# Cross attention without mask products: forbidden exponentials cleared after the fact on GpSimd and VectorE

## The chip, the cores and the metric

One core of a Trainium2 chip runs the whole kernel. The metric is the device time of one execution in microseconds. Engines are named as in the profile: PE is TensorE (PEld its weight loads), DVE is VectorE, ACT is ScalarE, POOL is GpSimd, SP is SyncE, whose queue issues nearly all transfers (SPq).

## The reference, cut to what matters

One layer of a decoder on 4 sequences of 1024 rows and 256 columns, f32: windowed self attention, cross attention to 77 context rows, and a quantized feed-forward part, each on the layer-normed input and added to it. The change is in the cross attention (16 heads of 16):

```
q = split(Q @ Wq.T + bq);  k = split(K @ Wk.T + bk);  v = split(V @ Wv.T + bv)
scores = einsum('bhqd,bhkd->bhqk', q, k) * 0.25
scores = where(mask == 0, -inf, scores)          # mask: (1024, 77) integers
out = einsum('bhqk,bhkd->bhqd', softmax(scores), v)
x = x + out @ Wo.T + bo
```

## The kernel before

Attention is cut into 16 jobs, `JOBS`: (self or cross, sequence, half of the heads), written S0a, X0a and so on. A job has two groups g of four heads. A group of a self job is 8 units of 128 keys, a group of a cross job 4 units of 256 queries (the 77 keys lie on the partitions), 64 cross units in all. For each group the kernel does this:

- *max*: a first product of queries by keys (`run_tensor`, L677) with the mask added by a further product with the identity (L679), and VectorE takes the negated row maxima (L1183; L1179 in self jobs). *rows*, *turnm*: the maxima are cut in three bf16 parts, turned, and sent by a transfer into three extra rows of the queries, so that the next product subtracts them.
- *score*: the second product, transposed (keys on partitions). For a unit of a cross job: for each pair z of heads two matmuls (L706) and then a mask product (L709), which adds -1e30 at forbidden places by multiplying `maskt` with the identity. Each unit fills two of the six PSUM banks.
- ScalarE takes the exponential of both banks at once (L978; self L974) into one of three buffers `pt`. In self jobs GpSimd then clears the half that causality forbids with an affine select (L1451); in cross jobs nothing follows.
- *val*: four matmuls with the values and a column of ones (L748; self L737), accumulated in the two remaining banks; then ScalarE moves them out (*evac*, L987), and the sums go through a gather, a reciprocal, a store and a wide load (*gather*, *invert* L1206, *store*, *widen*) to the scaling on VectorE (*scale*, L1216) and the output product (*out*, L759).

No engine chooses its next step at run time. `attention_order` writes one list of steps out by hand: each group has a period of 24.5 (self) or 9.6 (cross) units of planned time, and `PLACE` gives the fractions of the period between which the steps of a kind are spread. Steps that follow another (`follow`) are put `BEHIND` so many steps after it. `val` is put two units behind its score. Each engine runs the steps that concern it in the order of this list and waits on semaphores. `pool_steps` is GpSimd's share of the list, `banks_of` gives PSUM banks in turn, and `read_out` says which semaphore frees a bank. The cross keys and values of the next job are made in a step `xkeys` (L649 on TensorE, L1169 on VectorE, L1446 on GpSimd; the last two wait for the last `val` of the job two places earlier in `JOBS`) and in a `bulk` step of six transfers from `kparts` (L517), both under the place "keys x".

The mask itself is loaded once (*masks*, L1108 to L1113): `maskq` for the first product, and its transpose `maskt` for the second, both with 0 or -1e30.

## Time and profile before

| | us |
|---|---|
| median of 3 runs | 851.69 |
| lowest and highest | 844.95, 858.25 |
| span of the profiled execution | 849.0 |
| busy TensorE, VectorE, ScalarE, GpSimd | 684.6, 545.8, 415.1, 188.8 |
| cross scores run between | 300 and 701 |

The profiled execution is one run with the profiler on; its span goes from its first to its last instruction and no other time of it is given. A matmul's duration in the table is from start to modelled end; consecutive matmuls overlap, so that the start of the next one tells what a matmul holds TensorE for. An idle time is put down to the work that ended it.

### The profile page before, as it was taken

Reading aid. Unit: us, or ns where it says so; the run is one execution under the profiler, and the core shown is the slowest. Engines: PE = TensorE matmul, PEld = TensorE weight load, DVE = VectorE, ACT = ScalarE, POOL = GpSimd, SP = SyncE. Lnnn points to the kernel's source line nnn. Section 1 sums busy time; section 2 is a strip of 40 time slices with the busy share of each in tenths; the row PEclk is TensorE's granted clock in tenths of the full one; section 3 lists DMA queues with packets and bytes.
Section 4 is the critical chain, followed back from the end, with each engine's and each line's share of the span. In section 5 each row is a group of like instructions: output and inputs, shape, how many; then the busy total and the mean of one; then the engine's idle time right before and its main releaser. Section 6 shows DMA issues by size and latency. Waiting matters only on the chain.

```text
span 849.0 us, 14814 instructions
## 1 busy us (share of the span) xinstructions
PE 684.6 (81%) x5391; PEld 414.9 (49%) x5396; DVE 545.8 (64%) x975; ACT 415.1 (49%) x610; POOL 188.8 (22%) x231
## 2 busy tenths in 40 slices
PE   2579999989996998999979989897886784488565
PEld 1346565655653564556644644464543442233254
DVE  6277658866864456677636874556745651679996
ACT  2324665536463444555334446433343352399775
POOL 5002131312231120310113123002002000044436
PEclk9988999999997997999988989997998786699989
DMA  7534243502622153243222432331237112000013
GB/s 215 125 106 143 54 128 81 149 3 90 165 77 61 21 170 105 46 141 78 86 50 96 109 96 69 97 95 42 70 85 211 23 42 53 0 1 2 0 65 135
DMA packets 59557, 71.83 MB, mean 85 GB/s; under 512 B 25003, under 2 KB 36447, under 8 KB 59487
## 3 DMA queue, kind: packets, MB, share of 16 engines
q1 hardware_dynamic: 53391, 68.01, 29.2%
q10 hardware_dynamic: 6096, 2.88, 1.3%
q8 instruction: 44, 0.72, 0.4%
q14 instruction: 26, 0.21, 0.1%
HBM read 17.74 MB, written 4.72 MB: 26 GB/s over the span
## 4 chain that ended last, share of the span: by engine, by line
PE 49%; DVE 22%; issue 8%; ACT 7%; SPq 6%; DMA 6%; ACTq 1%; POOL 1%; POOLq 0%; DVEq 0%
PE banks L630 8%; PE banks L759 7%; PE banks L667 5%; PE banks L737 5%; DVE mneg L1179 4%; PE banks L699 4%; PE banks L640 3%; PE banks L748 3%; SPq L523 3%; PE banks L670 3%; DVE xn L1143 2%; SPq L517 2%; PE banks L706 2%; PE banks L709 2%; DVE tops L1358 2%
## 5 line engine op out<-in xcount | busy, mean ns | idle before, releaser
L1179 DVE TENSOR_REDUCE mneg<-banks 128x4 f32<-128x1024 f32 (+1 forms) x128 | 145.1, 1151 | 68.0 <-PE banks L670 67.5
L974 ACT ACTIVATE big<-banks 128x1024 f32<-128x1024 f32 (+1 forms) x128 | 123.0, 974 | 105.4 <-PE banks L699 101.7
L1451 POOL TENSOR_SCALAR_AFFINE_SELECT big<-big 128x512 f32<-128x512 f32 x128 | 83.1, 650 | 391.6 <-ACT big L974 390.9
L978 ACT ACTIVATE big<-banks 77x1024 f32<-77x1024 f32 x64 | 65.3, 1020 | 86.3 <-PE banks L709 81.8
L667 PE MATMUL banks<-big 96*128 96x256 bf16 (+1 forms) x512 | 94.5, 280 | 13.4 <-DMA big<-parts 9.8
L630 PE MATMUL banks<-xnT,weights 128*128 128x512 f32 x192 | 92.9, 617 | 3.9 <-ACT big L978 3.9
L699 PE MATMUL banks<-big 99*128 99x256 bf16 (+1 forms) x512 | 79.3, 280 | 13.3 <-DMA big<-m3t 5.7
L1183 DVE TENSOR_REDUCE mneg<-banks 128x8 f32<-128x616 f32 x64 | 50.3, 793 | 57.7 <-PE banks L679 57.6
L737 PE MATMUL banks<-big 128*17 128x256 f32 (+1 forms) x1152 | 79.0, 366 | 1.0 <-POOL big L1451 0.6
L670 PE MATMUL banks<-causal,identb 128*128 128x256 bf16 x256 | 72.9, 288 | 0.0
L667 PEld LDWEIGHTS banks<-big 96*128 96x128 bf16 x512 | 47.9, 103 | 45.9 <-issue 26.6
L699 PEld LDWEIGHTS banks<-big 99*128 99x128 bf16 x512 | 45.0, 101 | 48.3 <-issue 32.5
L803 PE MATMUL banks<-oe,weights 128*128 128x512 bf16 x187 | 46.8, 394 | 11.0 <-DVE big L1352 4.4
L630 PEld LDWEIGHTS banks<-xnT,weights 128*128 128x128 f32 x192 | 35.7, 197 | 38.1 <-issue 31.4
L677 PE MATMUL banks<-big 96*128 96x77 bf16 x512 | 43.1, 214 | 13.2 <-DMA big<-kparts 9.6
L706 PE MATMUL banks<-big 99*77 99x256 bf16 x256 | 51.1, 282 | 3.1 <-DVE big L1169 1.1
L677 PEld LDWEIGHTS banks<-big 96*128 96x128 bf16 x512 | 35.3, 108 | 32.9 <-issue 19.8
L709 PE MATMUL banks<-maskt,identb 77*77 77x512 bf16 x128 | 50.4, 394 | 0.0
L987 ACT COPY oe<-banks 128x512 f32<-128x512 f32 x64 | 37.2, 585 | 26.8 <-DMA oTx<-oe 10.9
L1224 DVE TENSOR_TENSOR xs<-banks,xs 128x512 f32<-128x512 f32 x32 | 22.1, 689 | 37.6 <-PE banks L759 37.6
L618 PE MATMUL banks<-ident,xn 128*128 128x128 f32 x128 | 23.7, 319 | 23.9 <-DVE xn L1143 23.5
L748 PE MATMUL banks<-big 77*17 77x256 f32 x512 | 42.7, 426 | 0.0
(155 smaller groups left out, 1163.8 us busy)
## 6 DMA issues: line engine op xcount, KB each, us to landing
big<-parts SPq DMA_DIRECT2D x282, 128.0 KB, 2.5
oc<-sums SPq DMA_DIRECT2D x16, 512.0 KB, 4.6
oTs<-oe SPq DMA_DIRECT2D x64, 64.0 KB, 2.3
out_dram<-oTs SPq DMA_DIRECT2D x16, 256.0 KB, 2.1
xs<-in_x_dram SPq DMA_DIRECT2D x3, 1024.0 KB, 5.8
big<-oe SPq DMA_DIRECT2D x32, 64.0 KB, 2.3
oTx<-oe SPq DMA_DIRECT2D x32, 64.0 KB, 2.3
big<-kparts SPq DMA_DIRECT2D x96, 9.6 KB, 1.8
```

Source lines behind the costliest of these rows:

```text
L630: t = e.matmul(bank(p), w[:, i, :], xnT[T][:, i, blk * 512:blk * 512 + 512], start=(i == 0), stop=(i == 1))
L667: e.matmul(bank(p, j)[:, i * 256 + lo * 128:i * 256 + 256], Q[0:96, hh, c * 128:c * 128 + 128], K[0:96, hh, (c - 1 + lo) * 128:(c + 1) * 1 ...
L670: t = e.matmul(bank(p, j).rearrange("p (s n) -> p s n", s=2)[:, :, 128:256], identb[:, :], causal[:, :].rearrange("p (a n) -> p a n", a=1) ...
L677: e.matmul(bank(p, j)[:, i * KX:i * KX + KX], Q[0:96, i, (c + j) * 128:(c + j) * 128 + 128], xks[r][0:96, i, :], start=(i == 0), stop=Fals ...
L699: t = e.matmul(bank(p, i // 2)[:, (i % 2) * 256:(i % 2) * 256 + n], ks[r][0:99, i, j * 128:j * 128 + 128], qs[r][0:99, i, j * 128:j * 128 ...
L706: e.matmul(bank(p, z)[0:KX, i * 256:i * 256 + 256], xks[r][0:99, 2 * z + i, :], qs[r][0:99, 2 * z + i, j * 256:j * 256 + 256], start=(i == ...
L709: t = e.matmul(bank(p, z)[0:KX, :].rearrange("p (i n) -> p i n", i=2), identb[0:KX, 0:KX], keep.to_broadcast([KX, 2, 256]), start=False, s ...
L737: t = e.matmul(acc[:, col // 512][32 * i:32 * i + 17, col % 512:col % 512 + z - a], va[f][:, j, 4 * g + i, :], P[:, i, a:z], start=new, st ...
L748: t = e.matmul(acc[:, j // 2][32 * i:32 * i + 17, (j % 2) * 256:(j % 2) * 256 + 256], xv[r][0:KX, i, 0:17], pt[u][0:KX, i * 256:i * 256 + ...
L974: e.activation(pt[u].rearrange("p (i n) -> p i n", i=4)[:, :, 0:n], pair(p).rearrange("p j (s n) -> p (j s) n", s=2)[:, :, 0:n], ACT.Exp, ...
L1179: e.tensor_reduce(M.rearrange("p (h c) -> p h c", h=4)[:, :, c], pair(p).rearrange("p j (s n) -> p (j s) n", s=2)[:, :, lo * 128:256], AX. ...
L1451: e.affine_select(out=P[:, :, 0:128], in_=P[:, :, 0:128], compare_op=ALU.is_ge, fill=0.0, base=0, pattern=[[0, 4], [1, 128]], channel_mult ...
```

## The change

The mask products of the second cross product go, and the scores of forbidden keys are no longer lowered. The exponentials of forbidden places, which can be large or infinite, are set to zero in the buffer: in two heads GpSimd multiplies the bits as integers with 0 or 1 (`keepi`), in the other two VectorE takes the minimum with 0 or 3e38 (`maskt`, with new contents). GpSimd's product is the score step in its list; VectorE's minimum is a new step "keep", put two steps behind the score. The value product now waits for both. The first product keeps its mask. The place "keys x" moves from before the start of a period to behind it. `keepi` takes 4 KB per partition, and the scratch for transfer descriptors is made smaller.

```diff
-         "bulk x": (0.192, 0.576), ... "keys x": (-0.198, -0.165), ...
+         "bulk x": (0.192, 0.576), ... "keys x": (0.02, 0.06), ...
 BEHIND = {...
-          "wturn": 2, "val": 2}
+          "wturn": 2, "val": 2, "keep": 2}
 def follow(s):
+    if k == "score" and s[1][0] == "x":
+        return ("keep", BEHIND["keep"], ("keep",) + s[1:])
 ...
+        keepi = sb("keepi", [128, S], I32)
 ...
 run_tensor, score:
-                        keep = maskt[0:KX, j * 256:j * 256 + 256].rearrange("p (a n) -> p a n", a=1)
                         for z in range(2):
                             for i in range(2):
-                                e.matmul(bank(p, z)[0:KX, i * 256:i * 256 + 256], xks[r][0:99, 2 * z + i, :],
-                                         qs[r][0:99, 2 * z + i, j * 256:j * 256 + 256], start=(i == 0), stop=False,
-                                         skip_group_check=True)
-                            t = e.matmul(bank(p, z)[0:KX, :].rearrange("p (i n) -> p i n", i=2), identb[0:KX, 0:KX],
-                                         keep.to_broadcast([KX, 2, 256]), start=False, stop=True, skip_group_check=True)
+                                t = e.matmul(bank(p, z)[0:KX, i * 256:i * 256 + 256], xks[r][0:99, 2 * z + i, :],
+                                             qs[r][0:99, 2 * z + i, j * 256:j * 256 + 256], start=(i == 0), stop=True,
+                                             skip_group_check=True)
 run_tensor, val of a cross job:
-                        e.wait_ge(a_exp, n_of["score", job, g, j])
+                        e.wait_ge(p_keep, n_cross[job, g, j])
+                        e.wait_ge(d_keep, n_of["keep", job, g, j])
 run_vector, masks:
-                    e.tensor_copy(maskt[0:KX, :], bank(p).bitcast(BF16)[0:KX, :]).then_inc(d_mask, 1)
+                    e.tensor_scalar(maskt[0:KX, :], bank(p).bitcast(BF16)[0:KX, :], 0.0, BIG, ALU.is_equal, ALU.mult
+                                    ).then_inc(d_mask, 1)
+                    e.tensor_scalar(keepi[0:KX, :], bank(p).bitcast(BF16)[0:KX, :], 0.0, None, ALU.is_equal
+                                    ).then_inc(d_mask, 1)
 run_vector:
+                elif k == "keep":
+                    _, job, g, j = s
+                    P = pt[pt_at[job, g, j]][0:KX, 512:1024].rearrange("p (i n) -> p i n", i=2)
+                    e.wait_ge(a_exp, n_of["score", job, g, j])
+                    e.wait_ge(d_mask, 2)
+                    e.tensor_tensor(P, P, maskt[0:KX, j * 256:j * 256 + 256].rearrange("p (a n) -> p a n", a=1).to_broadcast(
+                        [KX, 2, 256]), ALU.min).then_inc(d_keep, 1)
 run_gpsimd: "score" steps of cross jobs too
                     e.wait_ge(a_exp, n_of[s])
+                    if job[0] == "x":
+                        e.wait_ge(d_mask, 3)
+                        bits = P[0:KX, 0:2, :].bitcast(I32)
+                        keep = keepi[0:KX, j * 256:j * 256 + 256].rearrange("p (a n) -> p a n", a=1)
+                        e.tensor_tensor(bits, bits, keep.to_broadcast([KX, 2, 256]), ALU.mult).then_inc(p_keep, 1)
 kernel:
-    nc = _bacc.Bacc("TRN2", target_bir_lowering=False, num_devices=1)
+    nc = _bacc.Bacc("TRN2", target_bir_lowering=False, num_devices=1, dynamic_dma_scratch_size=1024)
```

## Rows read from the trace of the kernel before

**Rows 1.** The page, parts 1 and 4: busy us and share; the chain by engine.

```profile
PE 684.6 (81%) x5391; PEld 414.9 (49%) x5396; DVE 545.8 (64%) x975; ACT 415.1 (49%) x610; POOL 188.8 (22%) x231
...
PE 49%; DVE 22%; issue 8%; ACT 7%; SPq 6%; DMA 6%; ACTq 1%; POOL 1%; POOLq 0%; DVEq 0%
```

**Rows 2.** Groups by line and shape: count | busy us, mean ns | idle before.

```profile
L1451 POOL TENSOR_SCALAR_AFFINE_SELECT big<-big 128x512 f32<-128x512 f32 x128 | 83.1, 650 | 391.6 <-ACT big L974 390.9
...
L709 PE MATMUL banks<-maskt,identb 77*77 77x512 bf16 x128 | 50.4, 394 | 0.0
...
L1458 POOL TENSOR_TENSOR xs<-xs,big 128x512 f32<-128x512 f32 x16 | 21.1, 1319 | 1.3
```

**Rows 3.** Timeline of TensorE: start us, us, engine, line.

```profile
385.72 0.38 PE L709 MATMUL banks<-maskt,identb 77*77 77x512 bf16 x1
...
385.94 0.38 PE L706 MATMUL banks<-big 99*77 99x256 bf16 x2
```

**Rows 4.** The chain of waits, shares by line, of five stretches in order.

```profile
by line: SPq L523 16.7%; PE banks L667 12.3%; PE banks L630 9.6%; DMA big<-m3t 9.1%; PE banks L706 7.7%; PE banks L748 7.3%; PE banks L709 7.3%; DMA big<-parts 6.5%; PE banks L670 6.1%; PE banks L640 5.3%; issue 2.9%; PE banks L699 2.8%; AC
...
by line: PE banks L759 17.2%; PE banks L748 9.6%; PE banks L667 9.1%; PE banks L640 8.4%; PE banks L706 7.3%; PE banks L709 6.9%; PE banks L737 6.2%; PE banks L618 4.3%; PE banks L670 4.3%; PE banks L630 3.9%; PE banks L677 3.4%; DVE mneg L
...
by line: PE banks L667 11.7%; PE banks L640 10.9%; PE banks L706 10.3%; PE banks L748 10.3%; PE banks L630 10.1%; PE banks L709 9.0%; DMA big<-m3t 8.5%; PE banks L737 7.8%; PE banks L670 6.0%; PE banks L699 3.3%; PE banks L677 3.0%; PE bank
...
by line: PE banks L759 13.1%; SPq L523 12.3%; PE banks L748 8.6%; SPq L517 7.1%; issue 6.2%; PE banks L630 4.9%; PE banks L706 4.1%; PE banks L709 3.9%; DVE xn L1143 3.7%; ACT big L978 3.7%; SPq L535 3.5%; PE banks L677 3.5%; PE banks L679 
...
by line: PE banks L759 14.0%; DMA oc<-sums 12.0%; issue 6.9%; SPq L535 6.3%; SPq L517 4.7%; DMA sums<-ls 4.3%; SPq L523 4.0%; PE banks L706 3.8%; PE banks L709 3.4%; ACT big L978 3.4%; DMA ls<-oe 3.2%; DVE st L1229 3.1%; DMA oTx<-oe 3.0%; A
```

**Rows 5.** Windows: PE, PEld, DVE, ACT, POOL busy us, PE clock, DMA share, GB/s.

```profile
296.00:332.00 36.00, 31.89 (x286) 20.37 (x290) 20.10 (x34) 17.41 (x26) 7.29 (x8) 0.96 0.51 144
370.00:414.00 44.00, 42.42 (x354) 29.17 (x354) 27.40 (x52) 19.56 (x29) 3.57 (x4) 0.96 0.34 93
460.00:494.00 34.00, 31.66 (x290) 20.15 (x286) 25.85 (x45) 16.81 (x24) 8.61 (x8) 0.95 0.36 101
528.00:640.00 112.00, 94.29 (x788) 57.80 (x784) 65.13 (x139) 44.10 (x64) 14.81 (x20) 0.92 0.33 84
640.00:716.00 76.00, 47.57 (x359) 28.05 (x358) 35.86 (x82) 28.63 (x55) 3.54 (x4) 0.77 0.33 83
...
380.00:390.00 10.00, 10.00 (x98) 7.41 (x98) 9.33 (x21) 4.82 (x8) 1.67 (x1) 1.00 0.50 127
```

**Rows 6.** Timeline: cross exponentials (L978) and weight loads of value products (L748).

```profile
301.42 1.02 ACT L978 ACTIVATE big<-banks 77x1024 f32<-77x1024 f32 x1 [2.14 <-PE banks L709]
...
311.45 0.13 PEld L748 LDWEIGHTS banks<-big 77*17 77x17 f32 x8 [0.30 <-issue]
...
693.22 1.01 ACT L978 ACTIVATE big<-banks 77x1024 f32<-77x1024 f32 x1
...
694.28 0.13 PEld L748 LDWEIGHTS banks<-big 77*17 77x17 f32 x8 [0.49 <-ACT big L978]
...
702.47 1.03 ACT L978 ACTIVATE big<-banks 77x1024 f32<-77x1024 f32 x1
...
703.70 0.56 PEld L748 LDWEIGHTS banks<-big 77*17 77x17 f32 x16
```

**Rows 7.** Timeline: two-input operations of VectorE and GpSimd, alone and together.

```profile
326.51 1.22 DVE L1216 TENSOR_TENSOR oTs<-oTs,oc 128x1024 f32<-128x1024 f32 x1
...
638.43 1.71 DVE L1216 TENSOR_TENSOR big<-big,oc 128x1024 f32<-128x1024 f32 x1
...
639.13 2.13 POOL L1458 TENSOR_TENSOR xs<-xs,big 128x512 f32<-128x512 f32 x1
```

**Rows 8.** The table of waits: engine, line, released by: us, times, longest.

```profile
PE banks L677 <- DMA big<-kparts: 9.6, 2, 4.9
...
DVE big L1169 <- PE banks L748: 5.5, 3, 4.2
```

More of the change, by code:

```diff
@@ L43 @@
 BEHIND = {"scaled": 3, "turned": 3, "scaled 4": 0, "split": 1, "vmove": 0, "bulk": 13, "turnm": 3, "evac": 4,
-          "spread": 2, "gather": 2, "invert": 5, "store": 2, "widen": 8, "scale": 8, "wturn": 2, "val": 2}
+          "spread": 2, "gather": 2, "invert": 5, "store": 2, "widen": 8, "scale": 8, "wturn": 2, "val": 2, "keep": 2}
 def follow(s):
@@ L399, in build @@
         land_y = [sem(f"land_y{i}") for i in range(4)]
-        p_set, p_ones, p_mix, p_rstd, p_rstd3, p_one, p_sel, p_shift, p_wend = (
-            sem("p_" + n) for n in ("set", "ones", "mix", "rstd", "rstd3", "one", "sel", "shift", "wend"))
+        p_set, p_ones, p_mix, p_rstd, p_rstd3, p_one, p_sel, p_keep, p_shift, p_wend = (
+            sem("p_" + n) for n in ("set", "ones", "mix", "rstd", "rstd3", "one", "sel", "keep", "shift", "wend"))
         a_wqkv, a_turnw, a_keys, a_xnT, a_p0, a_p1, a_v, a_m3t, a_exp, a_evac, a_wb, a_wT, a_centre = (
@@ L404, in build @@
                                     "centre"))
-        d_set, d_ctx, d_mask, d_keys, d_clear, d_stat, d_ve, d_xn, d_rem, d_p2, d_xv, d_max, d_rows, d_inv, d_scale = (
-            sem("d_" + n) for n in ("set", "ctx", "mask", "keys", "clear", "stat", "ve", "xn", "rem", "p2", "xv", "max",
+        d_set, d_ctx, d_mask, d_keys, d_clear, d_stat, d_ve, d_xn, d_rem, d_p2, d_xv, d_max, d_keep, d_rows, d_inv, d_scale = (
+            sem("d_" + n) for n in ("set", "ctx", "mask", "keys", "clear", "stat", "ve", "xn", "rem", "p2", "xv", "max", "keep",
                                     "rows", "inv", "scale"))
@@ L440, in read_out @@
                     "xkeys": d_xv, "max": d_max, "turnm": a_m3t, "score": a_exp, "out": d_out}[k], {
-                        "turnw": 2 * n, "masks": 2 * n, "keys": 3 * n - 2, "xkeys": 2 * n}.get(k, n)
+                        "turnw": 2 * n, "masks": 3 * n, "keys": 3 * n - 2, "xkeys": 2 * n}.get(k, n)
         def w_done(s):
@@ L1404, in done @@
                 if k == "score":
-                    n -= n_cross[s[1:]]
-                return {"ones": p_ones, "mix": p_mix, "root": p_rstd, "xkeys": p_one, "score": p_sel, "shift": p_shift,
+                    x = n_cross[s[1:]]
+                    return (p_keep, x) if s[1][0] == "x" else (p_sel, n - x)
+                return {"ones": p_ones, "mix": p_mix, "root": p_rstd, "xkeys": p_one, "shift": p_shift,
                         "root3": p_rstd3, "wend": p_wend}[k], {"xkeys": 2 * n, "wend": 2}.get(k, n)
@@ L1422, in run_gpsimd @@
                 e.memset(va[f][:, :, :, 16:17], 1.0).then_inc(p_set, 1)
-            pool_steps = [s for s in plan if s[0] in ("ones", "mix", "root", "xkeys", "shift", "root3", "wend")
-                          or (s[0] == "score" and s[1][0] == "s")]
+            pool_steps = [s for s in plan if s[0] in ("ones", "mix", "root", "xkeys", "score", "shift", "root3", "wend")]
             for before, s in zip([None] + pool_steps, pool_steps):
```

6 lines of the change are left out of this document (4 added, 2 removed), and 2 rows, old and new, of the table PLACE.

## The prediction

> **What bounds the kernel now.** I read the page first: over the whole span TensorE is busy 81%, VectorE 64% and GpSimd 22%, and the chain that ended last is 49% TensorE, 22% VectorE [rows 1]. An average over stages does not say what the cross scores are worth, so I asked for the chain of waits in the five stretches in which cross scores run (296 to 332, 370 to 414, 460 to 494, 528 to 640, 640 to 716 us; 8, 8, 8, 27 and 13 of the 64 units of work, 302 us together). The reader is to see in them that the mask product L709 is 7.3, 6.9, 9.0, 3.9 and 3.4% of the chain [rows 4]: the first three stretches are nearly pure TensorE, the last two are mixed with DMA issues of SyncE (SPq L523, L517, L535) and landings. Then I looked at what is to take the work over: VectorE is busy 174 of these 302 us, and in its fullest 10 us 9.33 [rows 5].
>
> **The change part by part.**
>
> *Mask products removed (TensorE).* The table gives 50.4 us for 128 of them [rows 2], but matmuls overlap: L709 starts at 385.72 and the next matmul at 385.94, so one costs TensorE 0.22 us and all 128 cost 28.2 [rows 3]. Of this only what lies on the chain can shorten the end: 0.073 x 36 + 0.069 x 44 + 0.090 x 34 + 0.039 x 112 + 0.034 x 76 = 2.6 + 3.0 + 3.1 + 4.4 + 2.6 = 15.7 us [rows 4]. Term: -15.7; ends: 0 (everything hidden by the DMA issues that stand in the same chains) and -28.2.
>
> *Clearing on GpSimd, 64 products on 77x512 elements with two inputs from SBUF.* The trace has no integer product. Below stands the select of 512 elements with one input, 0.65 us, above the one two-input operation of 512 elements that was held up, 2.13 [rows 2, 7]. I take the two-input f32 form, 1.26 to 1.32 us [rows 2], since the change has its shape: 64 x 1.3 = 83 us on an engine that is busy 22% [rows 1]. Engine time there costs nothing; what costs is that it stands between the exponential (L978) and the product with the values (L748). That product is issued two units behind its score. Over the 64 pairs of L978 and L748 (first, a tight one and last in [rows 6]; the first load follows 9.0 us after its exponential) I took the time from the exponential's end to the first weight load that uses it: 57 of 64 have over 1.26 us and hide the product, 7 have less, the shortest 0.05 (exponential ends 694.23, load 694.28 [rows 6]). What is missing sums to 4.9 us. Each score shortened by 0.44 takes slack away from the pairs before it (about 1.5 scores lie between): 0.66 less each makes it 9.5. Delays of neighbours overlap, so: +6; ends 0 and 19 (the same sum at 1.95, the price of both halves in a row, below).
>
> *Clearing on VectorE, 64 minima on 77x512.* The row of 1024 columns takes 1.22 us undisturbed [rows 7], so half of it is about 0.69 with its fixed part. They are queued two steps behind the score on VectorE's in-order queue; behind each one wait the maxima (L1183, L1179) for which TensorE's six banks are held. So VectorE's added time counts by stretch. At 0.69 each, with VectorE filled to 0.93 as in its fullest window [rows 5], a stretch needs at least (busy + added)/0.93: 27.5, 35.4, 33.7, 90 and 48 us. Only the third is then over its new length (34.0 - 3.1 = 30.9), by 2.8.
>
> *The two halves at once.* Both wait for the same exponential. What the trace shows of such pairs: VectorE's product of two SBUF tensors took 1.71 instead of 1.22, and GpSimd's addition that began inside it took 2.13 instead of 1.26 [rows 7]: the second one in got through little while the first ran (0.87 of the 1.01 us that they overlap). So a pair that starts together ends after 0.69 + about 0.86 to 1.0 x 1.26, 1.8 to 1.95 us, and whichever was second carries it. I take the mean cost of a minimum to VectorE as up to 1.3, since it is in the middle of other work at 34 of the 64 ends of an exponential and then arrives late, when the product is partly done. At 1.3 the third stretch needs 39.0 (8.1 over), the others still fit: 32.8 against 33.4, 40.6 against 41.0, 107.8 against 107.6, 57 against 73.4. Term for VectorE: +5, between 2.8 and 8.1; ends: 0 and +43, which with the -15.7 makes the +27 of rival 2. The Trainium skill, "SBUF — State Buffer", section "Who interferes with whom", has a rule that speaks against this change: a VectorE instruction with two SBUF inputs and a GpSimd instruction that reads SBUF exclude each other for the whole instruction. By it each pair that meets takes the full sum of both durations, where the rows let some 0.1 us pass, and if all 64 met with VectorE second, rival 2's time would come out. The trace nearly agrees, with 0.87 of 1.01 us.
>
> *Cross keys later.* In the written order the step moves from 0.198 of a period's length (9.6 for cross, 24.5 for self, in the planner's us) before the period's start to 0.02 behind it: 2.1 later beside cross work, 5.3 beside self work. It is queued on four engines. VectorE's L1169 waits for the end of the value products, 5.5 us in its largest group [rows 8]; standing later it waits less, but it is also behind the minima: -1. The six key transfers per group of heads move behind other transfers of SyncE's queue; TensorE waited 9.6 us for such transfers, twice [rows 8]; hidden elsewhere, here by the same 2.1 to 5.3 more each at worst: +1; ends 0 and +7.4. GpSimd now takes cross scores in order, so a small reciprocal root or a shift may stand behind one product: +1 (ends 0, +4). The third mask operation of VectorE in the setup is one of some 0.7 us beside SyncE's loads and TensorE's first jobs: 0. The smaller scratch of DMA descriptors touches no queue of the trace, where all kernel transfers are issued by SyncE and ScalarE: 0.
>
> *Clock.* The granted clock is 0.96, 0.96, 0.95, 0.92 and 0.77 of full speed (means of the levels 2.4 and 1.2 GHz) [rows 5], lowest where TensorE waits most. New waits may cost one more stretch at 1.2 GHz and less work may bring one forward; ±5, in the range only.
>
> **Sum.** 849.0 - 15.7 + 6 + 5 - 1 + 1 + 1 = 845.3 us against the profiled span of 849.0. The three runs have a median of 851.69 and spread from 844.95 to 858.25, so the span lies 2.7 below the median; on the median's footing the sum is 848.
>
> **Rivals.**
> 1. *TensorE alone decides* (the chain's other parts were only filling its gaps): all 28.2 us go, +6 for the tight exponentials, no loss on VectorE: 851.7 - 28.2 + 6 = 829.5. For it: TensorE is busy 248 of 302 us [rows 5]. Against: the last two stretches, 188 of the 302 us, have 3.4 and 3.9% of L709 on the chain [rows 4]. Chance 0.13.
> 2. *VectorE becomes the bound, slower.* Every minimum is held behind the integer product and costs VectorE 1.95, 125 us in all. By (busy + added)/0.93 the stretches become 38.4, 46.2, 44.6, 126.7 and 73.4 us: +2.4, +2.2, +10.6, +14.7, -2.6, together +27.3, so 879. Place: the in-order VectorE queue in front of the maxima; it decides from a mean cost of 1.3 us a minimum. The rule of the Trainium skill, "SBUF — State Buffer", "Who interferes with whom", comes to this if GpSimd always gets in first. For it: two engines released by one semaphore; VectorE already 9.33 of 10 us full. Against: VectorE's waits for TensorE are part of its idle time and many exponentials end when GpSimd could be through before VectorE comes. With an integer product of 2 us instead of 1.3 it comes sooner. Chance 0.22, from 862 up.
> 3. *Nothing moves*: the chains run over SPq and DMA rows as soon as TensorE is shorter: 852 ± 3. Chance 0.13.
> 4. *The change doesn't do what it says*: an integer product that GpSimd executes much slower than the f32 form, 64 times over 3 us, with each value product waiting for it: above 900. Chance 0.02.
>
> **Numbers.** The forecast (0.50) has its own range of 838 to 860. Low end 832 takes in part of rival 1, high end 872 part of rival 2; 2 in 10 are left out. A measurement of this kernel can hardly tell less than 2%, 17 us, from no change. Faster than 834.7: most of rival 1 and a little of the forecast, 0.15. Slower than 868.7: most of rivals 2 and 4, 0.21. Within: 0.64.
>
> **What would show it.** In the profile after: no L709; TensorE's table total for the cross scores down by 50 us, its starts by 0.22 each. GpSimd +64 products of some 1.3 us, its total up by some 83 us. VectorE's minima: 0.69 where alone, up to 1.95 where both run; a mean above 1.3 and more idle time of TensorE behind L1183 and L1179 is rival 2. L748 waiting for GpSimd or for the minimum in some ten of 64 places, about 1 us each, is my second term; none says that slack grew. SPq L517 on the chain says that the later keys cost. I am wrong if the integer product is far from 1.3 us, or if VectorE meets it nearly always.

## The result: 5% slower, and the profile after

| | before | after |
|---|---|---|
| median of 4 runs each, us | 854.65 | 894.54 |
| lowest and highest | 844.95, 858.25 | 893.84, 895.72 |
| span of the profiled execution | 849.0 | 891.7 |
| mean granted clock of the span | 0.911 | 0.864 |

The ratio is 1.050, with a 95% interval of 1.043 to 1.057. The forecast of 848 us (832 to 872) was a little faster than before, and the kernel came out slower. An execution over 1.5% above the fastest of its kernel is left out of every ratio and every difference here, while medians and ranges given in brackets are of all executions.

The page of the kernel after, parts 1 and 2 (busy us and share by engine; tenths in 40 slices), for [rows 1]:

```profile
PE 690.7 (77%) x5263; PEld 413.5 (46%) x5268; DVE 614.0 (69%) x1040; ACT 416.2 (47%) x610; POOL 287.6 (32%) x295
...
PEclk9889999999997988999899799778665755789979
```

TensorE has 128 matmuls less and is busy 6 us longer; VectorE has 68 us more, GpSimd 99. The digits of the clock fall to 5, 6 and 7 from the 29th to the 35th slice. The same line on the page of the kernel before has 6 to 8 from the 31st to the 35th:

```profile
PEclk9988999999997997999988989997998786699989
```

The groups that the change made or touched, kernel after (line engine op, count | busy us, mean ns | idle before and releaser), for [rows 2]:

```profile
L1467 POOL TENSOR_TENSOR big<-big,keepi 77x512 int32<-77x512 int32 x64 | 95.5, 1492 | 169.0 <-ACT big L980 132.5
...
L1196 DVE TENSOR_TENSOR big<-big,maskt 77x512 f32<-77x512 f32 x64 | 57.2, 894 | 14.4 <-ACT big L980 14.4
L750 PE MATMUL banks<-big 77*17 77x256 f32 x512 | 52.8, 501 | 16.2 <-DVE big L1196 12.1
...
L709 PE MATMUL banks<-big 99*77 99x256 bf16 x256 | 49.9, 331 | 5.1 <-DVE mneg L1188 2.9
```

L709 is now the score itself; the mask product behind it is gone. Windows, first the kernel before between its first and its last cross exponential (301.4 to 702.5), columns as in [rows 5]:

```profile
301.40:702.50 401.10, 344.23 (x2855) 209.90 (x2851) 249.46 (x497) 180.05 (x268) 63.96 (x84) 0.90 0.34 89
```

The same of the kernel after, and below it the stretches that hold as many cross units as the five of [rows 5] (8, 8, 8, 27 and 13):

```profile
301.10:743.20 442.10, 348.96 (x2733) 208.68 (x2734) 315.46 (x559) 180.98 (x267) 160.98 (x148) 0.82 0.30 81
296.00:337.00 41.00, 31.19 (x281) 18.97 (x270) 29.21 (x40) 17.39 (x26) 18.92 (x17) 0.90 0.43 124
374.00:422.00 48.00, 41.24 (x354) 28.15 (x355) 36.48 (x64) 19.43 (x30) 16.06 (x13) 0.96 0.32 90
467.00:510.00 43.00, 34.31 (x274) 20.02 (x276) 34.96 (x58) 17.08 (x24) 20.53 (x17) 0.82 0.29 78
544.00:681.00 137.00, 101.48 (x734) 60.58 (x730) 95.44 (x169) 45.62 (x65) 49.67 (x44) 0.75 0.28 74
681.00:758.00 77.00, 50.01 (x323) 27.46 (x323) 46.40 (x90) 28.13 (x54) 32.02 (x20) 0.57 0.28 67
```

This is the whole loss: between the two exponentials 41.0 of the 42.7 us of the spans. The stretches went from 36, 44, 34, 112 and 76 us to 41, 48, 43, 137 and 77. VectorE is not full in any of them: 71, 76, 81, 70 and 60%.

**Where the 41.0 us are.** Length less TensorE's busy time is its idle time: 401.1 - 344.2 = 56.9 before, 442.1 - 349.0 = 93.1 after, +36.3. The other 4.7 is busy time. It hides two large terms. The mean clock tells how long TensorE was granted the lower of its two levels (1.2 instead of 2.4 GHz; a mean of 0.90 is 20% of the time, 0.82 is 36%). From the clock records themselves it is 78.5 us before and 161.5 after. Taking busy time at the lower level as half as much work, the work at full clock fell by 27.3 us, and 32.1 us came back because so much of it ran at the lower clock. So: -27.3 work, +36.3 idle, +32.1 clock.

**What TensorE waits for.** The table of waits of TensorE between the two exponentials, kernel before (engine, line, released by: us, times, longest):

```profile
PE banks L759 <- DVE oTx L1216: 8.6, 2, 8.3
PE banks L687 <- DVE m L1199: 7.2, 6, 2.0
...
PE banks L618 <- DVE xn L1143: 4.7, 8, 1.3
```

And the kernel after:

```profile
PE banks L691 <- DVE m L1211: 20.6, 11, 4.1
PE banks L750 <- DVE big L1196: 12.1, 8, 2.4
PE banks L773 <- ACT big L1009: 8.3, 7, 2.6
PE banks L671 <- DVE mneg L1184: 7.2, 11, 1.2
...
PE banks L750 <- POOL big L1467: 2.9, 2, 1.6
```

All rows of this view added up by the releasing engine: VectorE 30.8 us before, 62.7 after; GpSimd 0 and 3.2; ScalarE 13.2 and 11.3; transfers 11.6 and 10.4. The new idle time is VectorE's (+31.9), and most of it stands in places that the change did not touch. The largest is the transposition of the row maxima (L691, before L687). It needs four small VectorE instructions in a row (two copies and two subtractions of 128x32, each waiting for the one before, L1205 to L1211). Two things delay them. They stand in one queue with the minima, and they are themselves held while GpSimd works: of the 84 of them between the two exponentials, the 21 that began while a two-input GpSimd instruction ran took 0.68 us on average and up to 1.25, the other 63 took 0.22. In sum they took 28.3 us instead of 18.3. The new wait of the value products for the minimum is 12.1 us, 8 times.

**The pairs.** A timeline of the kernel after, the first cross unit (start, us, engine, line):

```profile
301.12 1.02 ACT L980 ACTIVATE big<-banks 77x1024 f32<-77x1024 f32 x1 [1.56 <-PE banks L709]
...
302.28 1.26 POOL L1467 TENSOR_TENSOR big<-big,keepi 77x512 int32<-77x512 int32 x1 [2.22 <-ACT big L980]
302.42 1.67 DVE L1196 TENSOR_TENSOR big<-big,maskt 77x512 f32<-77x512 f32 x1
```

The product comes 0.14 us ahead and takes its 1.26 us; the minimum takes 1.67 instead of 0.68. And a unit of the kernel after in which they do not meet, but the minimum stands behind other work:

```profile
392.08 1.02 ACT L980 ACTIVATE big<-banks 77x1024 f32<-77x1024 f32 x1 [2.52 <-PE banks L709]
...
393.24 1.65 POOL L1467 TENSOR_TENSOR big<-big,keepi 77x512 int32<-77x512 int32 x1 [2.33 <-ACT big L980]
...
393.87 2.15 DVE L1148 TENSOR_SCALAR xn<-xs,mv,rstd 128x256 f32<-128x256 f32 x4
...
395.93 1.22 DVE L1184 TENSOR_REDUCE mneg<-banks 128x4 f32<-128x1024 f32 x1
...
397.06 0.68 DVE L1196 TENSOR_TENSOR big<-big,maskt 77x512 f32<-77x512 f32 x1
397.66 1.22 DVE L1184 TENSOR_REDUCE mneg<-banks 128x4 f32<-128x1024 f32 x1
...
397.89 0.63 PE L750 MATMUL banks<-big 77*17 77x256 f32 x8 [1.48 <-DVE big L1196]
```

The exponential ended at 393.10, the product with the integers at 394.89. The minimum came at 397.06, after a normalisation and a maximum, and TensorE stood 1.48 us for it. Over all 64 minima: 39 took 0.67 to 0.69 us, and 25, all begun while a two-input GpSimd instruction was running, took 1.23 on average and up to 1.76.

### The profile page after: what moved, and what is told of

Its sections match the earlier page's. It is cut to its first block and busy times, and to the rows that moved or that the text cites. A ratio compares the mean times of both kernels' runs of the same rounds, so it can differ in the third digit from the quotient of the medians.

```text
span 891.7 us, 14850 instructions
## 1 busy us (share of the span) xinstructions
PE 690.7 (77%) x5263; PEld 413.5 (46%) x5268; DVE 614.0 (69%) x1040; ACT 416.2 (47%) x610; POOL 287.6 (32%) x295
## 5 line engine op out<-in xcount | busy, mean ns | idle before, releaser
L1467 POOL TENSOR_TENSOR big<-big,keepi 77x512 int32<-77x512 int32 x64 | 95.5, 1492 | 169.0 <-ACT big L980 132.5
L671 PE MATMUL banks<-big 96*128 96x256 bf16 (+1 forms) x512 | 95.9, 284 | 19.4 <-DMA big<-parts 10.4
L634 PE MATMUL banks<-xnT,weights 128*128 128x512 f32 x192 | 95.2, 631 | 0.5 <-DVE big L1159 0.5
L738 PE MATMUL banks<-big 128*17 128x256 f32 (+1 forms) x1152 | 77.2, 357 | 1.3 <-POOL big L1469 0.8
L671 PEld LDWEIGHTS banks<-big 96*128 96x128 bf16 x512 | 47.8, 104 | 54.0 <-issue 28.4
L1196 DVE TENSOR_TENSOR big<-big,maskt 77x512 f32<-77x512 f32 x64 | 57.2, 894 | 14.4 <-ACT big L980 14.4
L750 PE MATMUL banks<-big 77*17 77x256 f32 x512 | 52.8, 501 | 16.2 <-DVE big L1196 12.1
L681 PE MATMUL banks<-big 96*128 96x77 bf16 x512 | 47.6, 229 | 19.6 <-DMA big<-kparts 11.0
L681 PEld LDWEIGHTS banks<-big 96*128 96x128 bf16 x512 | 38.9, 117 | 41.7 <-issue 27.4
L709 PE MATMUL banks<-big 99*77 99x256 bf16 x256 | 49.9, 331 | 5.1 <-DVE mneg L1188 2.9
L683 PE MATMUL banks<-maskq,identb 128*128 128x308 bf16 x128 | 47.0, 371 | 0.0
```

The source lines that it names most:

```text
L634: t = e.matmul(bank(p), w[:, i, :], xnT[T][:, i, blk * 512:blk * 512 + 512], start=(i == 0), stop=(i == 1))
L671: e.matmul(bank(p, j)[:, i * 256 + lo * 128:i * 256 + 256], Q[0:96, hh, c * 128:c * 128 + 128], K[0:96, hh, (c - 1 + lo) * 128:(c + 1) * 1 ...
L681: e.matmul(bank(p, j)[:, i * KX:i * KX + KX], Q[0:96, i, (c + j) * 128:(c + j) * 128 + 128], xks[r][0:96, i, :], start=(i == 0), stop=Fals ...
L738: t = e.matmul(acc[:, col // 512][32 * i:32 * i + 17, col % 512:col % 512 + z - a], va[f][:, j, 4 * g + i, :], P[:, i, a:z], start=new, st ...
L1196: e.tensor_tensor(P, P, maskt[0:KX, j * 256:j * 256 + 256].rearrange("p (a n) -> p a n", a=1).to_broadcast([KX, 2, 256]), ALU.min).then_in ...
L1467: e.tensor_tensor(bits, bits, keep.to_broadcast([KX, 2, 256]), ALU.mult).then_inc(p_keep, 1)
```

## The experiments

"After" and "before" name the two kernels. Each ratio is to before, run on the same chip. The medians of before, counted as said above, were 850.6 us beside e1 to e4, 850.9 beside e5 to e8, 848.3 beside e10 to e13 and 848.9 beside e9 and e14 to e16. First the parts of the change one by one.

**Both clears out** (e1). From after, GpSimd's products and VectorE's minima are left out, and the value product waits for the exponential:

```diff
-        return ("keep", BEHIND["keep"], ("keep",) + s[1:])
+        return None
...
-                        e.wait_ge(p_keep, n_cross[job, g, j])
-                        e.wait_ge(d_keep, n_of["keep", job, g, j])
+                        e.wait_ge(a_exp, n_of["score", job, g, j])
... (and cross scores leave pool_steps)
```

> The changed kernel with both clears left out (the exponentials at forbidden places stay, the value product waits for ScalarE only); mask products gone, cross keys at their new place. Theory Q (the minimum stands late in VectorE's in-order queue and holds the value products): all of the loss goes and the mask products' 15.7 us show, 830 to 840 us, granted clock 0.90 or more. Theory C (less matmul work alone lets the clock fall: half clock 244 us after against 154 before): the clock stays at 0.88 or lower and the time is 865 us or more. Theory K (keys later): 870 us or more, TensorE waiting for key transfers.

Measured: 853.34 us (847.79 to 858.1), ratio 1.003 (0.999 to 1.007). The clears are what makes after slow; without them it is no faster than before, and none of the three numbers expected came true. The forbidden exponentials stay, so the result of e1 and e2 is not the layer's.

**Only the mask products removed** (e2). As the last, with the keys where they were. It keeps two small parts of the change, the third mask operation of the setup and the smaller scratch:

```diff
-         "keys x": (0.02, 0.06)
+         "keys x": (-0.198, -0.165)
```

> As the run before it, with the cross keys back at their old place: nothing but the mask products is taken from the kernel before. Q: within 5 us of the kernel without clears and new keys. K: faster than that one by 10 us or more. C: granted clock under 0.89 and no gain on the kernel before; Q: 12 to 20 us faster than before.

Measured: 847.42 us (842.49 to 850.38), ratio 0.997 (0.993 to 1.001): 3.2 us where 15.7 were forecast, at most 5.8 by the interval. The 12 to 20 us of theory Q did not come. Its window between the two exponentials, in one of its shortest executions (842.6):

```profile
296.90:693.00 396.10, 326.14 (x2728) 199.63 (x2725) 249.03 (x497) 179.64 (x268) 64.25 (x85) 0.87 0.34 90
```

Work at full clock is 26.6 us less than before, as in after. Idle time is 70.0 (13.1 more), and the lower clock takes 99.6 us instead of 78.5, which costs 8.5. So 26.6 us of removed matmuls shorten the stretch by 5.0. TensorE now waits 39.1 us for VectorE instead of 30.8: part of what was work is a wait for the same VectorE results. The lower clock shows in all executions: the mean granted clock of the span was 0.882 to 0.897 in the ten of e2 and 0.897 to 0.919 in the nineteen of before. The chain's 15.7 us were about five times too much, the 28.2 us from the starts about nine times.

**Only the keys moved** (e3). From before:

```diff
-         "keys x": (-0.198, -0.165)
+         "keys x": (0.02, 0.06)
```

> The kernel before with the cross keys at their new place and nothing else. K: 15 us or more slower than before. Q and C: within 7 us of before.

Measured: 848.72, 862.56, 863.17 and 863.42 us. With three of four far above the fourth no ratio is given, and this run decides nothing: it lies between 2 us less and 13 more. No cause is read from its profile, which is of one of the three. The pair above, e1 against e2, has ten executions of each on one chip, and their means differ by 6.6 us, with a 95% interval of some 4 to 9. So in the kernel without mask products and clears the later keys cost some 6 us; in the kernel before it is open.

**Mask products and clears together** (e4). After, with the mask product put back behind each score (the scores are masked twice):

```diff
-                                t = e.matmul(..., start=(i == 0), stop=True, skip_group_check=True)
+                                e.matmul(..., start=(i == 0), stop=False, skip_group_check=True)
+                            t = e.matmul(bank(p, z)[0:KX, :]..., identb[0:KX, 0:KX],
+                                         keep.to_broadcast([KX, 2, 256]), start=False, stop=True, ...)
```

> The changed kernel with the mask products put back beside both clears, which then clear zeros. C: the matmul work holds the clock at 0.90 or more and the kernel is faster than the changed one, under 880 us. Q: the waits stay and 128 products of 0.22 us come on top where TensorE is on the path: 890 to 910 us, clock near 0.87.

Measured: 901.13 us (899.51 to 905.46), ratio 1.059 (1.053 to 1.064): 6.6 over after. The window holds 27 us more work than after, and 73.2 us of idle time instead of 93.1. What the mask products cost in front of the clears is, within the noise, what they cost without them, some 3 to 7 us.

**GpSimd's products alone** (e5; after without the minima; VectorE's two heads stay uncleared):

```diff
-        return ("keep", BEHIND["keep"], ("keep",) + s[1:])
+        return None
...
-                        e.wait_ge(d_keep, n_of["keep", job, g, j])
```

> The changed kernel without the minima (two of four heads keep their forbidden exponentials; the value product waits for GpSimd's product alone). The two clears together cost 41 us (894.5 against 853.3 without them). Theory Q (the minimum's late place in VectorE's in-order queue and the wait on it): most of the 41 is gone, 853 to 865 us. Theory B (the two engines exclude each other while reading SBUF, and VectorE's time grows by the lock): also gone, so this run alone doesn't part them. Theory G (GpSimd's 1.26 us between exponential and value product, with its own in-order queue): over 870 us.

**VectorE's minima alone** (e6; after without the products; GpSimd's two heads stay uncleared):

```diff
-            pool_steps = [s for s in plan if s[0] in (..., "xkeys", "score", "shift", "root3", "wend")]
+            pool_steps = [s for s in plan if s[0] in (..., "xkeys", "shift", "root3", "wend")
+                          or (s[0] == "score" and s[1][0] == "s")]
...
-                        e.wait_ge(p_keep, n_cross[job, g, j])
```

> The changed kernel without the integer products (the other two heads keep their forbidden exponentials). Q: the loss stays nearly whole, 880 to 894 us, since the minimum stands where it stood. B: without GpSimd there is nothing to exclude, 853 to 868 us. G: 853 to 868 us.

Measured: products alone 870.64 us (865.64 to 870.93), ratio 1.022 (1.018 to 1.027), 17.3 over e1. Minima alone 862.66 (859.65 to 870.1), ratio 1.015 (1.008 to 1.023), 9.3 over e1. The two add up to 26.6; together, in after, they cost 41.2. So 14.6 us (13 by the ratios, and some 10 either way) come from their being there at the same time. The group of the minima in the kernel with minima alone:

```profile
L1195 DVE TENSOR_TENSOR big<-big,maskt 77x512 f32<-77x512 f32 x64 | 44.1, 690 | 15.9 <-ACT big L979 15.9
```

The product alone adds no instruction to VectorE, and still VectorE's busy time between the two exponentials grows. The window of e1 and below it that of e5 (columns as in [rows 5], VectorE is the third):

```profile
297.46:707.81 410.35, 332.96 (x2728) 202.38 (x2724) 248.34 (x497) 179.94 (x267) 63.17 (x85) 0.85 0.32 87
297.17:720.87 423.70, 340.27 (x2727) 204.09 (x2724) 266.88 (x497) 179.88 (x267) 145.97 (x148) 0.84 0.32 84
```

The same 497 instructions take 18.5 us more. The four small ones of the row maxima account for 10.0 of it: the 17 of 84 that began while a two-input GpSimd instruction ran took 0.77 us on average, the others 0.22. TensorE's wait for the last of them rose from 7.7 to 15.5 us, and with the minima alone (e6) only to 9.1. Reductions and operations with an input in PSUM kept their times (128x4 from 128x1024: 1.21 us inside and outside). So a good part of the product's price is that it slows what VectorE already had to do; TensorE waited only 5.2 us for the product itself.

**One product for all four heads** (e7), on GpSimd, no minima. It computes the whole result:

```diff
-                    bits = P[0:KX, 0:2, :].bitcast(I32)
+                    bits = P[0:KX, 0:4, :].bitcast(I32)
```

> One integer product of 77x1024 on GpSimd clears all four heads, no minima: the full result. Its duration should be near 2.5 us, twice 1.26. Q: 2.5 us exceed the gap to the value product in about half of the 64 units, but no VectorE step is in the way: 860 to 875 us. G: worse than the changed kernel, over 895 us. B: 860 or less.

Measured: 910.93 us (899.97 to 915.55), ratio 1.067 (1.059 to 1.075). The group, and the first of the four small VectorE instructions in e1 and in e7 (shortest/median/longest in ns, over the whole span):

```profile
L1466 POOL TENSOR_TENSOR big<-big,keepi 77x1024 int32<-77x1024 int32 x64 | 152.6, 2384 | 137.7 <-ACT big L979 110.8 <-issue 19.1 <-DVE ve L1247 4.8
...
L1204 DVE CAST m<-mneg x32: 117/174/535, 58.4 to 694.6; 128x32 bf16<-128x32 f32 x32
L1204 DVE CAST m<-mneg x32: 119/174/2335, 58.4 to 732.0; 128x32 bf16<-128x32 f32 x32
```

GpSimd alone, with no minimum in VectorE's queue, costs 56 us over e1 once its instruction is 2.38 us long. VectorE, without one instruction more than in e1, is busy 297.3 us between the exponentials instead of 248.3. The four small instructions took 41.7 us instead of 18.1, and TensorE waited 27.7 us for the last of them instead of 7.7, 9.4 for the product itself. Splitting the work was the better choice of the two.

Next, what the clears cost through waits and what through the time of the engine.

**The minimum without its waits** (e8). After, but the minimum works on a tile of its own and nobody waits for it, nor it for an exponential; the products stay. Two heads stay uncleared:

```diff
-                    P = pt[pt_at[job, g, j]][0:KX, 512:1024]...
-                    e.wait_ge(a_exp, n_of["score", job, g, j])
...
+                    P = idle[0:KX, :]...
+                    e.wait_ge(d_keep, n_of[s] - 1)
-                        e.wait_ge(d_keep, n_of["keep", job, g, j])     (value product)
```

> The changed kernel with each minimum at its place on a tile of its own: it waits for no exponential and nothing waits for it (two heads stay uncleared); VectorE's time and the meeting with GpSimd's product stay, both waits are gone. Q: near the kernel with GpSimd alone, within 8 us of it. B: near the changed kernel, over 880 us.

Measured: 896.28 us (891.91 to 897.41), ratio 1.053 (1.048 to 1.058): the same as after. The minima took 895 ns on average. The 12.1 us of L750 waiting for L1196 are gone and nothing is won: TensorE has 93.6 us of idle time instead of 93.1, and its wait for the integer product at the same place rose from 2.9 to 8.1. Against e5, which has no minima, unread minima cost 25.6 us.

**The minimum two steps earlier** (e9), directly behind its score:

```diff
-"val": 2, "keep": 2}
+"val": 2, "keep": 0}
```

> The changed kernel with the minimum directly behind its score in the order rather than two steps later. In the changed kernel the minimum starts 0.03 to 7.8 us after its exponential's end because VectorE is behind in its queue; now VectorE waits for the exponential with maxima queued behind. Theory W2 (late minima hold the value products): 875 to 885 us. Theory V with L (time on VectorE and exclusion, not the place): within 8 us of the changed kernel, or slower, since more pairs meet at the exponential's end.

Measured: 893.38 us (890.95 to 899.84), ratio 1.054 (1.046 to 1.062). VectorE now waits for the exponential at this place, 44.0 us in 33 places instead of 14.4 in 8 (table of waits, this kernel), with the maxima behind it, and the time is that of after:

```profile
DVE big L1196 <- ACT big L980: 44.0, 33, 5.4
```

**Idle copies of the clears in the kernel before** (e11, e12, e13). The minimum on a tile of its own (waits for the exponential, nobody waits for it); the integer product likewise; both. The result is the whole one, and the scratch is the smaller one of after:

```diff
+                elif k == "keep":
+                    e.wait_ge(a_exp, n_of["score", job, g, j])
+                    e.wait_ge(d_keep, n_of[s])
+                    P = idle[0:KX, 0:512]...
+                    e.tensor_tensor(P, P, maskt[0:KX, ...], ALU.min).then_inc(d_keep, 1)
...
+                        bits = idlei[0:KX, :]...
+                        e.tensor_tensor(bits, bits, idlek[0:KX, :]..., ALU.mult).then_inc(p_keep, 1)
```

> The kernel before, mask products and key place untouched, with the minimum added at its place after the wait for the exponential, on a tile of its own, so that nothing waits for it. V: 8 to 12 us slower than before, like the minimum in the changed kernel. L: the same, since GpSimd does nothing new. Theory W (the value products' waits are the cost): within 3 us of before.

> The kernel before with the integer product added on tiles of its own after the wait for the exponential; nothing waits for it but GpSimd's own queue. W (the 17 us of the product were the value product's wait): within 3 us of before. L, widened (the product holds up VectorE's other two-port and two-input work): 8 to 17 us slower than before.

> The kernel before with both operations added on tiles of their own, no value product waiting. If time and exclusion are the cost (V with L), 26 to 41 us slower than before, more than the two single ones together. W: under 12 us slower.

Measured: minimum 860.96 us (859.34 to 872.75), ratio 1.015 (1.008 to 1.021); product 858.1 (853.38 to 862.18), 1.012 (1.004 to 1.020); both 881.58 (873.72 to 890.16), 1.043 (1.033 to 1.053). In us over the before of their job (848.3, from four executions): about +13, +10, +33. Again some 11 us are there only when both are. No value product waits for any of it, so some 30 of the 41 us of the clears are the bare presence of the instructions. For the product alone 8 to 17 us had been expected if it holds up VectorE's other operations, and the trace of e12 shows just that: TensorE waits 0.3 us for GpSimd between the exponentials and VectorE 1.0 as before, but VectorE is busy 266.4 us instead of 249.5 with the same 497 instructions. Both groups and the window of the kernel with both:

```profile
L1474 POOL TENSOR_TENSOR idlei<-idlei,idlek 77x512 int32<-77x512 int32 x64 | 98.3, 1535 | 155.1 <-ACT big L985 154.1
L1200 DVE TENSOR_TENSOR idle<-idle,maskt 77x512 f32<-77x512 f32 x64 | 56.0, 875 | 11.9 <-ACT big L985 11.8
...
296.70:723.20 426.50, 362.09 (x2851) 217.00 (x2848) 309.42 (x560) 181.12 (x268) 163.43 (x148) 0.86 0.31 84
```

The stretch is 25.4 us longer than before, with VectorE at 73% of it. TensorE's idle time is 64.4, 7.5 more, and 17.9 is busy time, nearly all of it by the clock (116.8 us at the lower level instead of 78.5, which costs 17.2). So most of what this execution, the shortest of four, is longer by comes through the clock.

Then the meeting of the two.

**A reduction in the minimum's place** (e10). The same 512 columns, the same waits, but one input from SBUF; two heads stay uncleared:

```diff
-                    e.tensor_tensor(P, P, maskt[0:KX, ...].to_broadcast([KX, 2, 256]), ALU.min).then_inc(d_keep, 1)
+                    e.tensor_reduce(idle[0:KX, 0:2], P, AX.X, ALU.max).then_inc(d_keep, 1)
```

> The changed kernel with each minimum replaced by a reduction of the same 512 columns (one SBUF input, waits as before, two heads stay uncleared). Its duration should be 0.65 to 0.70 us whatever GpSimd does. Theory L (mutual exclusion of the pair is what makes both together cost 41 us where 17 and 9 were the single costs): 15 us less than the changed kernel, 875 to 884 us. Theory V (VectorE's plain time in front of the maxima): no difference, 888 us or more.

Measured: 880.6 us (875.35 to 883.77), ratio 1.038 (1.030 to 1.045), 13.9 under after. Its two groups:

```profile
L1468 POOL TENSOR_TENSOR big<-big,keepi 77x512 int32<-77x512 int32 x64 | 88.0, 1375 | 167.8 <-ACT big L981 129.9 <-issue 29.7 <-DVE ve L1249 5.4
...
L1198 DVE TENSOR_REDUCE idle<-big 77x2 f32<-77x512 f32 x64 | 43.1, 674 | 15.1 <-ACT big L981 15.1
```

24 of the 64 reductions began while a two-input GpSimd instruction ran, and every one took 0.62 to 0.68 us. With two inputs, the minima that began so took 1.23. VectorE has 17 us less to do between the exponentials (298.5 against 315.5), waits of TensorE for VectorE fell from 62.7 to 52.3, and 14 us of the time are back (10 by the ratios). The three ways to the meeting's price agree within their noise: 13 to 15 us (e5 and e6), 11 (e11 to e13), 10 to 14 (e10).

**The minimum behind the product** (e15). After, with one wait more in front of the minimum, so that a pair does not meet:

```diff
                     e.wait_ge(a_exp, n_of["score", job, g, j])
+                    e.wait_ge(p_keep, n_cross[job, g, j])
```

> The changed kernel with the minimum also waiting for GpSimd's product of the same unit, full result. The pair can no longer meet, so a minimum takes 0.68 us whenever its product alone was the partner. Theory L (exclusion): VectorE's busy time falls by up to 14 us, but it now waits instead of being held: 890 to 900 us, no gain, since a held instruction and a waiting one block the queue alike. If the exclusion cost came from GpSimd being slowed: 880 us or less.

Measured: 906.29 us (902.95 to 908.75), ratio 1.067 (1.058 to 1.075), 12 over after and over the 890 to 900 expected. The minima still took 893 ns on average: 16 of them began while another two-input GpSimd instruction ran and took 1.5 us on average. The wait in VectorE's queue is paid in full and the meetings are not avoided.

**No meeting, but VectorE ahead of the exponential** (e16). For VectorE's two heads the mask is added to the scores in PSUM before the exponential. It computes the whole result:

```diff
-                    P = pt[pt_at[job, g, j]][0:KX, 512:1024]...
-                    e.wait_ge(a_exp, n_of["score", job, g, j])
-                    e.tensor_tensor(P, P, maskt..., ALU.min)
+                    P = bank(at_bank["score", job, g, j][0], 1)[0:KX, :]...
+                    e.wait_ge(t_score, n_of["score", job, g, j])
+                    e.tensor_tensor(P, P, maskt..., ALU.add)
+                        e.wait_ge(d_keep, n_of["keep", job, g, j])     (exponential)
```

> Full result: two heads by the integer product as in the changed kernel; in the other two VectorE adds the mask (0 or -1e30) to the scores in PSUM, right behind the score and before the exponential. One input is in PSUM, so by theory L it cannot exclude GpSimd's reads: near 0.7 us each with GpSimd busy. L: like the kernel with a reduction for the minimum (880 us) or better, 868 to 885 us. If VectorE's place in front of the exponential matters more: over 894 us.

Measured: 902.71 us (892.48 to 908.59), ratio 1.060 (1.049 to 1.071). Its two groups, and the wait that it made:

```profile
L1468 POOL TENSOR_TENSOR big<-big,keepi 77x512 int32<-77x512 int32 x64 | 81.1, 1268 | 205.2 <-ACT big L982 157.6 <-issue 44.6 <-DVE xn L1149 2.5
L1197 DVE TENSOR_TENSOR banks<-banks,maskt 77x512 f32<-77x512 f32 x64 | 43.9, 689 | 18.0 <-PE banks L711 17.4 <-issue 0.2
...
ACT big L982 <- DVE banks L1197: 141.9, 51, 9.6
```

Neither of the pair is held by the other any more (1268 and 689 ns, the times of the lone instructions). The small copies and subtractions still are: the 14 that began inside a two-input GpSimd instruction took 0.70 us. But now ScalarE stands 141.9 us for VectorE, in 51 of 64 places, and everything behind the exponential is late.

Last, the clock.

**Filler for TensorE** (e14). After, with four products of 512 columns, whose result is overwritten, ahead of each cross score:

```diff
+                        for z in range(2):
+                            for _ in range(2):
+                                e.matmul(bank(p, z)[0:KX, :], identb[0:KX, 0:KX], maskf[0:KX, 0:512],
+                                         start=True, stop=True, skip_group_check=True)
```

> The changed kernel with four products of 512 columns (identity by a constant tile) put before each cross score into its own banks, where the score then overwrites them: 256 products, 56 us of full-clock matmul work, twice what the mask products were. Between the first and the last cross exponential the changed kernel has 93 us without a matmul and 161 us at half clock. Theory C (too little matmul work lets the clock fall): half-clock time falls under 120 us and the kernel gains or loses little, 885 to 900 us. Theory I (the clock falls where TensorE waits, whatever the work): half-clock time stays at 150 us or more and most of the 56 us shows, 915 to 940 us.

Measured: 912.83 us (909.62 to 915.26), ratio 1.075 (1.068 to 1.083), 18 over after. The window:

```profile
299.00:762.50 463.50, 404.32 (x2977) 237.49 (x2974) 310.82 (x559) 181.23 (x267) 167.84 (x148) 0.84 0.29 77
```

The work at full clock is 54.1 us more than in after, and the stretch 21.4 longer. Idle time fell from 93.1 to 59.2 (34 us of the filler ran where TensorE had waited), and waits for VectorE from 62.7 to 33.4. The lower clock still takes 147.2 us of 161.5. Neither theory's number was met (147.2 lies just under the 150 of theory I, 912.8 us under its 915), but the clock did not come back with the work, so it is not mended by a few more matmuls. Nor does it follow the idle time alone: e14 has as little of it as before (59.2 and 56.9 us) and nearly twice the time at the lower level.

## Why the prediction was wrong

The forecast gave the clears +11 us (+6 and +5) and the products' removal -15.7. Measured, in medians: -3.2 for the mask products, +5.9 for the keys, +17.3 for GpSimd's product, +9.3 for the minimum, +14.6 for both at once: 850.6 to 894.5. This is a sum of differences from separate jobs: the terms for the products, the minima and their meeting carry some 6 to 10 us each way. The first step (e2, e4) and the last (e10, e13) rest on more than one kernel.

Point by point:

1. **Mask products.** The work was right (forecast 28.2, measured 27.3 at full clock). What it is worth was not: the share of the chain [rows 4] promised 15.7, e2 gave 3.2 (at most 5.8 by its interval). A chain names what ended last in one execution. When its piece is taken away, another chain of nearly the same length ends last: in e2 TensorE's idle time grew by 13.1 us, 8.3 of them waits for VectorE, and the time at the lower clock by 21.1.
2. **Duration of the integer product.** Right: 1.26 us alone, 1.29 on average in e5. Rival 4 is out.
3. **The failed step: "Engine time there costs nothing" for GpSimd, and for VectorE "a stretch needs at least (busy + added)/0.93".** For GpSimd the prediction priced only the wait of the value products. The product's 83 us lie on an engine that is busy 22%, but it holds many of VectorE's copies and two-input operations that begin while it runs, also those that the kernel before had: 18.5 us more of VectorE's time in e5, 49.0 in e7, and a product that nobody reads costs 10 us (e12). The prediction saw this holding, but counted it only for the minimum beside its product. For VectorE, both sentences take an engine's added time as free until it is full. After's stretches would need 29.2/0.93 = 31.4, 39.2, 37.6, 102.6 and 49.9 us by that rule and took 41, 48, 43, 137 and 77: not one is bound by it, and still four of them grew by 4 to 25 us. VectorE at 47 to 76% of a stretch [rows 5] already delays what TensorE waits for, since its work comes in chains (a maximum, then four small dependent instructions, then TensorE's transposition), not as a heap that may be done at any time. Idle copies that nobody waits for cost +13, +10 and, together, +33 (e11 to e13): this shows it without any wait of the change.
4. **The two halves at once.** The mechanism was seen and right: held minima of up to 1.76 us (forecast pair 1.8 to 1.95). The measured price is 10 to 15 us, three ways (e13, e5 with e6, e10). The mean of the minima, 0.89, stayed far under the 1.3 from which the rival was to decide: that point followed from the rule of step 3 and fell with it. So the prediction's own signs of being wrong, a product far from 1.3 us or a meeting nearly always, did not appear: 25 of 64 minima met. The Trainium skill, "SBUF — State Buffer", section "Who interferes with whom", says that a VectorE instruction with at most one SBUF input, outside the two-port modes, does not contend with GpSimd; e10 (a reduction of one input: never over 0.68 us) and e16 (scores from PSUM: 689 ns) agree.
5. **Latency behind the exponential.** Forecast +6 for 7 tight pairs. The rows show 12.1 us for the minimum in 8 places and 2.9 for the product in 2: ten places, as forecast, at 1.5 us each. But taking the minimum's waits away won nothing (e8: 896.3), which I read as others of the same length standing behind them. A product that is waited for (e5) costs 17 us and one that is not (e12) 10; the difference is within the noise.
6. **Keys.** Forecast 0 in all; the pair e1 and e2 says +6 (4 to 9) without mask products and clears. In the kernel before, e3 lies between -2 and +13. The cause is open.
7. **Clock.** Left at ±5 for the range. It is +32 of the 41 us of the profiled stretch, beside +36 of idle time. In the stretches of the kernel after it is 0.96 where TensorE is busy 86% and 0.57 where it is busy 65%, so it is lowest where TensorE waits most. But waits alone do not give it: e14 has the idle time of before and 147.2 us at the lower level, and in e13 7.5 us more of idle time go with 38.3 us more at that level.

Rival 2 (VectorE decides, 879) was the nearest in place and sign, with a chance of 0.22, but its price came from the wrong term: 68 us more on a VectorE that is busy 69%, not 125 us on a full one.

What stays open: how the 32 us of the lower clock share out among the causes (e14 shows only that work alone does not bring them back), and how the later keys cost what they do. No version that was run beats the kernel before by more than its interval (e2, the lowest, is at 0.997 with 0.993 to 1.001).

## What to carry to other kernels

Before you move work to an engine that is "only" 60% busy, ask which engine waits for it and in how long a chain of small steps: an idle copy of the new instruction in the old kernel, on a tile that nobody reads, gave most of its price in one run (33 of 41 us). Do not take a share of the chain for what a removal brings; here it was five times too much. A two-input operation on GpSimd is not beside VectorE's work but partly in its place: look at the mean times of VectorE's other instructions, the small copies above all, not only at the new pair. Two clears with two SBUF inputs each, side by side on VectorE and GpSimd, are not parallel. A reduction, or an input from PSUM, was not held, but the version that used this stood in front of the exponential and lost more than it won (e16).

## What the runs showed of the hardware

- GpSimd's product of int32 takes 1.26 us for 77x512 with two inputs, no more than its f32 addition of 128x512 (1.32 on average [rows 2]); 77x1024 takes 2.38 on average.
- A VectorE reduction of one SBUF input (0.67 us) begun inside a two-input GpSimd instruction is not held (24 of 24); a minimum of two inputs is: 1.23 us on average, up to 1.76, instead of 0.68.
- Of VectorE's copies and subtractions of 128x32 (0.22 us) the 24 of 84 begun inside a two-input GpSimd instruction in e7 took 1.17 us on average and up to 2.34; reductions, batch-norm statistics and operations with an input from PSUM kept their times.
- Removing 26.6 us of matmuls raised the time at the lower of the two clock levels (1.2 instead of 2.4 GHz) from 78.5 to 99.6 us; adding 54.1 us in front of the same waits lowered it only from 161.5 to 147.2.
